# One block and one list of steps for the linear layer, the routing and the keys and values of a four-stage transformer kernel

## What is computed

```python
x = x + linear(layernorm(x), mask, weight, bias)      # weight (512 x 512) in 32x32 blocks; a block counts if its mask has a one
x = x + routed(layernorm(x), router, router_bias, expert_bias)
x = x + attention(layernorm(x), Wq, Wk_down, Wv_down, Wk_up, Wv_up, Wo)   # 32 query heads, 8 key heads, causal
x = x + feed_forward(layernorm(x), gate, up, down)

def routed(h):                                        # 64 experts, the 8 best are kept
    scores = softmax(h @ router.T + router_bias)
    w, idx = top_k(scores, 8)
    w_dense = zeros(T, 64).at[idx].add(w)
    return h * w.sum() + w_dense @ expert_bias
```

## Time and profile before

| | before |
|---|---|
| median of 3 runs | 1710.38 us |
| the profiled execution's own time | 1713.57 us |
| its span | 1711.8 us |
| PE busy | 1649.8 us (96%) |
| DVE / ACT / POOL busy | 1177.9 / 928.2 / 817.9 us |
| DMA | 114.99 MB, mean 67 GB/s |
| first linear matmul / last one over | 20.61 us / about 73.5 us |
| first routing transposes on PE | 79.39 us |
| first Z task on PE | 138.23 us |
| first matmul of the attention | 296.23 us |

### The profile page before, as it was taken

One profiled execution on the slowest core, in us unless ns is written; L12 is line 12 of the kernel. 1 busy time (PEld: TensorE's weight loads), 2 busy tenths in 40 slices (PEclk: granted clock), 3 DMA queues, 4 the chain that ended last, 5 costly groups with the idle time before them and its releaser, 6 DMA issues. The chain is left out here.

```text
span 1711.8 us, 26527 instructions
## 1 busy us (share of the span) xinstructions
PE 1649.8 (96%) x8298; PEld 1377.9 (80%) x8298; DVE 1177.9 (69%) x3102; ACT 928.2 (54%) x2456; POOL 817.9 (48%) x1203
## 2 busy tenths in 40 slices
PE   5878999999999999999999999999999899999999
PEld 4667897788888888888888888888888788877887
DVE  6775324767767767767767767776777677877776
ACT  3464435566556657647556656656656453424432
POOL 4633002445346346346346346445446198718752
PEclk9889999999999999999999999999999999999999
DMA  5200555211111111124111111111111022003111
GB/s 158 78 1 1 197 192 205 71 38 50 62 38 50 62 38 50 62 87 173 62 38 43 62 44 38 51 56 44 50 40 48 32 72 64 32 25 123 50 50 50
DMA packets 61338, 114.99 MB, mean 67 GB/s; under 512 B 5456, under 2 KB 23888, under 8 KB 57104
## 3 DMA queue, kind: packets, MB, share of 16 engines
q1 hardware_dynamic: 60304, 112.74, 19.9%
q10 hardware_dynamic: 896, 0.56, 0.2%
HBM read 84.97 MB, written 28.31 MB: 66 GB/s over the span
## 5 line engine op out<-in xcount | busy, mean ns | idle before, releaser
L1769 PE MATMUL ps_q<-kv_w_hi,o_hi 128*128 128x512 f32 x512 | 205.6, 402 | 3.0 <-DVE o_lo L131 3.0
L1769 PE MATMUL ps_q<-kv_w_lo,o_hi 128*128 128x512 f32 x512 | 201.3, 393 | 0.0
L1769 PE MATMUL ps_q<-kv_w_hi,o_lo 128*128 128x512 f32 x512 | 201.1, 393 | 0.0
L131 POOL TENSOR_TENSOR kv_w_lo<-w_raw,kv_w_hi 128x512 fp32r<-128x512 f32 x128 | 163.1, 1291 | 58.0 <-ACT kv_w_hi L126 58.0
L1711 PE MATMUL ps_q<-h_hi,kv_w_hi 128*128 128x512 f32 x448 | 182.3, 407 | 3.3 <-PEq L1056 1.4
L1711 PE MATMUL ps_q<-h_hi,kv_w_lo 128*128 128x512 f32 x448 | 175.3, 391 | 0.0
L1711 PE MATMUL ps_q<-h_lo,kv_w_hi 128*128 128x512 f32 x448 | 175.2, 391 | 0.0
L126 ACT ACTIVATE kv_w_hi<-w_raw 128x512 fp32r<-128x512 f32 (+1 forms) x240 | 126.6, 566 | 64.3 <-POOL w_raw L472 62.1
L126 ACT ACTIVATE o_hi<-ps_o 128x512 fp32r<-128x512 f32 x128 | 76.2, 595 | 130.0 <-PE ps_o L1751 129.9
L1354 ACT ACTIVATE prob<-prob,neg_max 128x128 f32<-128x128 f32 x256 | 100.3, 392 | 84.8 <-DVE neg_max L1511 84.7
L1298 POOL TENSOR_SCALAR prob<-prob,inv_sum 128x128 f32<-128x128 f32 x256 | 95.2, 372 | 106.0 <-DVE inv_sum L1516 105.8
(11 more groups left out here) (240 smaller groups left out, 4886.0 us busy)
## 6 DMA issues: line engine op xcount, KB each, us to landing
w_raw<-in_wq_g SPq DMA_DIRECT2D x16, 1024.0 KB, 4.8
w_raw<-in_wo_g SPq DMA_DIRECT2D x16, 1024.0 KB, 4.8
k_scratch<-kv_stage SPq DMA_DIRECT2D x32, 256.0 KB, 2.4
v_scratch<-kv_stage SPq DMA_DIRECT2D x32, 256.0 KB, 2.1
k_raw<-k_scratch SPq DMA_DIRECT2D x32, 256.0 KB, 3.4
v_raw<-v_scratch SPq DMA_DIRECT2D x32, 256.0 KB, 3.8
f_gate_raw<-in_gate_c SPq DMA_DIRECT2D x10, 512.0 KB, 4.8
f_up_raw<-in_up_c SPq DMA_DIRECT2D x10, 512.0 KB, 3.7
```

Of the source, the lines that this page charges most:

```text
L131: return dve.tensor_tensor(parts[LO], src, parts[HI].bitcast(F32), ALU.subtract)
L1769: done = pe.matmul(ps_q[:, half, :], o[b][i][:, half, h, :], wo[j][:, h, :], start=(h == 0 and m == 0), stop=(h == GROUP - 1 and m == 2))
```

## The change

- The linear layer becomes a class (`SparseLinear`), and linear layer, routing, keys and values are issued in one block (`first_stages`) from one list of steps, `head_steps`. Step s holds linear step s, routing step i = s - 6 (`FIRST_ROUTED`), piece p = s - 7 of the key and value weights, and some kv tasks. `ROUTED_GAP` is 0, so the routing's tiles follow each other without a pause. There are 31 steps.
- Within a step each engine does its linear part first, then the routing's, then the piece, then the tasks.
- The first tasks come at routing step 17 instead of 16, in groups of 2, 2, 3, 2, 2, 2, 3, 2: 18 tasks stand beside the routing instead of 9. They use banks 0 to 3, which the linear layer had.
- The start is written out by hand for tiles 0 and 1 (`pe_start`, `act_start`, `dve_start`, `pool_start`): tiles 0 and 1 are normalized and transposed among the steps that prepare the weight. The loads are issued in another order, all on SP: x tile 0, four mask chunks, x 1, four weight chunks, x 2, bias, x 3, the router's three, the other x tiles, then the pieces.
- The transposed linear tokens are kept in the room of `h3` instead of two buffers of their own.
- The pieces are 24 of 256 columns instead of 16 of 384, and POOL makes their low parts instead of DVE. DVE makes no `neg_mean` any more; the shift is one POOL instruction with the mean and the factor -1. The variance for the second norm moves from DVE to POOL, which had that for the third norm already.
- `weight_sum` and `combined` (two DVE instructions) become two POOL instructions.
- The operand sums of the attention's query product start at task V 0 of the first half instead of K 4, and steps 4 to 7 stand at the Z tasks of the second half. Stores of operand steps 3, 4 and 5 move behind those of `store_blocks`. The 32 K and V results of the first half are staged in `query.raw`, which is also the room of z, so ACT's first copy of the second half waits until all have been stored.

```diff
+FIRST_ROUTED = 6
+ROUTED_GAP = 0
+FIRST_PIECE = 7
...
+def head_steps():
+    ready = TILES // 2 + RoutedBias.DEPTH
+    group = (2, 2, 3, 2, 2, 2, 3) + (2,) * (RoutedBias.STEPS - ready - 7)
+    steps, n = [], 0
+    for s in range(FIRST_ROUTED + RoutedBias.STEPS):
+        i = s - FIRST_ROUTED
+        count = group[i - ready] if i >= ready else 0
+        steps.append((s, i, s - FIRST_PIECE, range(n, n + count)))
+        n += count
+    return steps, n
...
+                linear.pool_start(pool)
+                for s, i, p, _ in steps:
+                    if s >= 2:
+                        linear.pool_body(pool, s)
+                    if i == 0:
+                        routed.set_constants(pool, linear)
+                    routed.pool_body(pool, i)
+                    if 0 <= p < KV_PIECES:
+                        piece_lo_part(pool, p)
...
+    def pool_body(self, pool, i):
+        if 0 <= i - 2 < TILES:
+            t = i - 2
+            pool.wait_ge(self.h_done, t + 1)
+            pool.tensor_tensor(tile_of(self.x, t), tile_of(self.x, t), self.bias[:, :], ALU.add).then_inc(self.xb_done, 1)
+        if 0 <= i - 5 < TILES:
+            self.ln_next.variance(pool, i - 5)
+            self.ln_next.power(pool, i - 5)
+        if 2 <= i < TILES:
+            self.ln.power(pool, i)
...
     def power(self, pool, t):
         pool.wait_ge(self.ve_done, t + 1)
-        pool.tensor_tensor(self.factor(t, 0), self.ve[:, bass.ds(t, 1)], self.half, ALU.pow).then_inc(self.rstd_done, 1)
+        pool.tensor_tensor(self.factor(t, 0), self.ve[:, t:t + 1], self.half, ALU.pow).then_inc(self.rstd_done, 1)
         pool.wait_ge(self.rstd_done, t + 1)
-        pool.tensor_tensor(self.factor(t, 1), self.neg_mean[:, bass.ds(t, 1)], self.factor(t, 0), ALU.mult).then_inc(self.shift_done, 1)
+        pool.tensor_scalar(self.factor(t, 1), self.mv[:, t, 0:1], self.factor(t, 0), -1.0, ALU.mult, ALU.mult).then_inc(self.shift_done, 1)
...
-            dve.tensor_tensor(self.weight_sum[:, odd:odd + 1], self.top_sum[:, odd:odd + 1], self.inv_total[:, bass.ds(t3, 1)], ALU.mult).then_inc(self.sum_done, 1)
...
-            dve.scalar_tensor_tensor(self.combined[:, odd, :], self.ln.factors[:, bass.ds(t3, 1), :].rearrange("p t n -> p (t n)"),
-                                     self.weight_sum[:, odd:odd + 1], self.one_zero[:, :], ALU.mult, ALU.add).then_inc(self.combined_done, 1)
...
+            pool.tensor_scalar(self.combined[:, t % 2, :], self.ln.factors[:, t, :], self.top_sum[:, t % 2:t % 2 + 1],
+                               self.inv_total[:, t:t + 1], ALU.mult, ALU.mult).then_inc(self.scaled_factors, 1)
+            pool.wait_ge(self.scaled_factors, t + 1)
+            pool.tensor_scalar(self.combined[:, t % 2, 0:1], self.combined[:, t % 2, 0:1], 1.0, None, ALU.add).then_inc(self.combined_done, 1)
...
+                        if (quad, a) == (1, 0):
+                            for done in stored:
+                                act.wait_ge(done, 16 * (STAGED // STAGES))
```

More of the change, by code:

```diff
@@ L1064, in _ @@
             def _(sp):
+                linear.load(sp, lambda eng: weights.load(eng, *router_sources))
+                sp.wait_ge(linear.w_lo_done, KC)
+                for p in range(KV_PIECES):
+                    load_piece(sp, p)
                 for k, n in enumerate(stage_order):
@@ L1119, in task @@
                         operands.step_hi(act, step_at[n])
[L1121 removed]
+                linear.act_start(act)
+                for s, i, p, now in steps:
+                    if s >= 3:
+                        linear.act_body(act, s)
+                    if i == 0:
+                        act.wait_ge(linear.w_lo_done, KC)
+                    routed.act_body(act, i)
+                    if 0 <= p < KV_PIECES:
+                        piece_hi_part(act, p)
+                    for n in now:
+                        task(n)
+                for n in range(paired, len(tasks)):
+                    task(n)
             @block.vector
             def _(dve):
[L1125 removed]
                 def task(n):
@@ L1138, in task @@
                             dve.wait_ge(routed.lo_done, TILES)
+                            dve.wait_ge(piece_lo, KV_PIECES)
                         operands.step_sum(dve, step_at[n])
-                interleaved(dve, routed.dve_body, task)
+                linear.dve_start(dve)
+                for s, i, _, now in steps:
+                    if s >= 2:
+                        linear.dve_body(dve, s)
+                    if i == 0:
+                        routed.await_constants(dve)
+                    routed.dve_body(dve, i)
+                    for n in now:
+                        task(n)
+                for n in range(paired, len(tasks)):
+                    task(n)
             @block.tensor
             def _(pe):
-                routed.await_constants(pe)
+                awaited = set()
                 def task(n):
                     kind, quad, a, b = tasks[n]
+                    if kind in pieces_of and kind not in awaited:
+                        awaited.add(kind)
+                        pe.wait_ge(piece_lo, pieces_of[kind])
                     freed(pe, n)
@@ L1177, in task @@
                     last.then_inc(task_done, 1)
-                interleaved(pe, routed.pe_body, task)
+                linear.pe_start(pe)
+                for s, i, _, now in steps:
+                    if s >= 3:
+                        linear.pe_body(pe, s)
+                    if i == 0:
+                        routed.await_constants(pe)
+                        pe.wait_ge(linear.on_done, 1)
+                    routed.pe_body(pe, i)
+                    for n in now:
+                        task(n)
+                for n in range(paired, len(tasks)):
+                    task(n)
     return [(stored[k], 16 * (len(stage_order) // STAGES)) for k in range(STAGES)]
```

772 lines of the change are left out of this document (392 added, 380 removed).

## The result

| | before | after |
|---|---|---|
| median | 1710.26 us (4 runs, 1709.73 to 1714.35) | 1680.23 us (4 runs, 1679.63 to 1682.08) |
| ratio, 95% interval | | 0.9821 [0.9804, 0.9837] |
| span of the profiled execution | 1711.8 us | 1678.0 us |
| PE busy | 1649.8 us | 1631.0 us |
| first Z task on PE | 138.23 us | 121.53 us |

Runs of the kernel before fall near 1710 or near 1714.5 us; one of them that took 9347 us and one of e13 that took 3311 us are left out of all medians here.

A forecast was written before the change was run, and what follows sets the result against it. PE, busy 96% of the span, bounds the kernel, so the head pays only where PE idles or runs slowly. Step 22 ends 18.4 us earlier, step 23 loses 1.3, net 17: median 1710.38 to 1693.5, range 1685 to 1703.

The forecast's parts named there:

- So from 138.23 on the head is PE's own work, the same in both kernels: From the first Z task at 138.23 us on: PE's work unchanged, so only how early PE stands there counts.
- C and K tasks come two and three at a time ... which I cost at nothing: Behind step 23, tasks and routing sharing PE: grouped tasks on four banks change nothing, 1 us either way.
- Step 23, 1.3 us lost: Routing step without tasks ahead of the first Z: PE has 2.3 us of work, DVE 3.5, so 1.3 is lost.
- The common steps: Linear and routing work sharing steps: full steps 6.6 us each, 3 us added for waits, step 22 ending at 119.3.
- The start: Tiles 0 and 1: tile 1's linear matmuls end at 27.5 us, before 29.03, still at 0.43 apiece.
- POOL as the bound of the full steps: Steps 13 to 15: POOL becomes the slowest engine, 6.6 us a step, busy over 90%.
- A common step wins almost nothing; what is won is in the seams: Full common steps: 6.6 us, where linear layer and routing apart took 3.2 + 3.7 = 6.9.
- Hidden costs at 0: Second half's stores, ACT's wait at the first Z copy, and loads: cost 0; without cover 3 for operand stores, 2 for ACT.
- Rival C: Chance 0.09: slack is better, POOL's lines pack closer and the start is 3 us earlier; gain 25, 1685.
- D: Rival, chance 0.04: the kernel gets slower; its sign is a clock of 0.50 beyond 40 us.
- B: Rival, chance 0.14: in-order waiting adds 0.75 to each of steps 7 to 18; gain 8, 1702.
- E: Rival, chance 0.03: gain given back at the attention's start by operands or stores arriving last; 1710.

The follow-up runs named there:

- e13: Changed kernel with two more small DVE instructions in each routing step, results unused; 1679.4 us, 0.9803 of the kernel before.
- e4: Changed kernel with both address edits undone (small attention tiles first, HEAD_FILL = 40), leaving the schedule alone; 1687.7 us, 0.9858 of the kernel before.
- e7: Changed kernel with one key-and-value task behind each of routing steps 17 to 24 instead of 2 or 3; 1681.0 us, 0.9810 of the kernel before.
- e5: Changed kernel with POOL's two memsets of the routing's constants in step 3 instead of step 6; 1678.0 us, 0.9795 of the kernel before.
- e9: e5 with the 24 weight pieces moved to steps where POOL has time, none in 13 to 15 and 19 to 22; 1674.8 us, 0.9771 of before.
- e6: Changed kernel with FIRST_ROUTED = 21 instead of 6, so routing starts after the linear layer's last tile; 1703.2 us, 0.9941 of the kernel before.
- e3: Changed kernel with HEAD_FILL = 40 instead of 32, first-stage tiles behind it 32 bytes higher; 1683.8 us, 0.9838 of the kernel before.
- e12: Kernel before, own schedule, with attention's small tiles last and 224 bytes of filling aligning first-stage tiles to 512 bytes; 1701.4 us, 0.9934 of before.
- e10: Changed kernel with 64 bytes of filling ahead of prob_t and 64 more ahead of o; 1689.9 us (one run).
- e2: Changed kernel with the attention edit undone, three small tiles ahead of prob_t again; 1685.3 us, 0.9848 of the kernel before.
- e11: Changed kernel with 256 bytes of filling ahead of prob_t and 32 more ahead of o; 1686.1 us (one run).

## Why the prediction was wrong, step by step

- **"So from 138.23 on the head is PE's own work, the same in both kernels"** is the step that failed, and with it the unspoken term of nothing for the attention behind the head. The same instructions are not the same work: their operands' addresses moved. It cost the forecast 7.5 us (e4; 6 to 11 by the other ways of taking it), 2.4 in K and V and 5 in the attention. The edits of `HEAD_FILL` and in `attention` were there to be read, and neither was looked at.
- **"C and K tasks come two and three at a time ... which I cost at nothing"**: the 3.7 us of idle time of before, all waits for h_lo, went. e7 gives 2.2 of them to the groups; the other 1.5 have no experiment.
- **Step 23, 1.3 us lost**: 0.8, a wait for h1t.
- **The common steps**: right within 1 us in the sum (118.3 against 119.3), by luck: the errors cancel, and the first Z alone varies by 3 us with the clock. The start was over at 25.7 instead of 27.5 (24.2 where the granted clock of tile 1 was 1.00). Its terms for PE are those of the earlier trace rows: 29.03 - 25.83 = 3.2 us for a linear tile, 5.9 with a routing step's 2.7, and 0.43 us from matmul to matmul in tile 0, where the profile of before has a granted clock of 1.00 (20.60 to 25.80), so that no run shows why they are not 0.23 apart. In the changed kernel tile 1's matmuls are 0.43 apart from 22.19 to 23.47 and 0.23 from 24.30 on. The wait for the constants, which the diff shows on POOL in step 6, was overlooked and costs 2.3 us (e5). Steps 13 to 18 took 36.0 us instead of 37.3, since POOL's lead carried PE through the first two. Steps 19 to 22 took 18.1 instead of 15.9.
- **POOL as the bound of the full steps**: right (e9), 6.87 against 6.6.
- **"A common step wins almost nothing; what is won is in the seams"**: half right. By the estimate under e6, some 12 of 21 us go to the hole and the half clock, and 9 to the common steps: PE's steps 13 to 18 took 6.0 us each, where linear layer and routing apart took 6.9.
- **Hidden costs at 0**: right; no wait for a store or a load appears on PE behind the first Z.
- Rival C gave the nearest time, 1685. Half of its reason did come: the start was 1.8 us earlier than forecast, 3.3 where the granted clock was 1.00. The other half did not, since POOL's lines packed no closer, and the rest of its gain came from the addresses. D stood at 0.04; its sign, a clock of 0.50 for more than 40 us, did not come. For some us the clock did fall: from 33 to 40 us the granted clock is 0.76, behind the 2.25 us wait, and from 106 to 110 us 0.57. B and E did not appear.

The terms add up: 17 + 1.0 + 4.2 = 22.2 against 22.5 measured for the schedule (e4), and 7.5 for the addresses. With the schedule alone the time is 1687.7, inside the range; the addresses took it out. Without the idle time that went, they would not have done so: 1693.5 - 7.5 = 1686.

## What to carry to other kernels

A change that adds, drops or reorders allocations moves every tile behind them: compare the start addresses of TensorE's operands before calling a stage unchanged, and keep them on multiples of 512 bytes, which were fast in K, V and the attention's products (227 to 228 ns from matmul to matmul, against 230 to 233.3) and made no gain in the linear layer of the old schedule (256 was tried once, 228.6 ns). Overlap two stages whose bounds lie on different engines, then count the engine that collects the small work, step by step, and put what can wait (here the pieces) in the steps in which that engine is ahead. A one-time job in a list of steps, such as setting constants, belongs where its engine is idle, not at the step that first needs it.

## What the runs showed of the hardware

- In K, V, the product with prob_t and the output product, all back-to-back matmuls of 128x512 in fp32r, one follows the last after 227 to 228 ns when both operands begin on a multiple of 512 bytes (228.6 in the one case of 256), and after 230 to 233.3 ns when one of them, moving or stationary, begins 32, 64, 128 or 192 bytes behind a multiple of 256: 1.1 to 2.8%. Why is open. The linear layer's matmuls follow it in the changed kernel (229.2 ns, and 233.0 in e3 with the weight alone 32 bytes off), but not in the schedule before (229.8 with both operands off, 230.9 with both on in e12). Z's matmuls, whose tokens lie eight apart, take 245 ns in both kernels, with both operands on multiples of 1024.
- The granted clock of PE fell to 0.50 behind an idle time of 2.25 us in some executions and not in others. In the changed kernel's trace it is 0.50 from 35.80 to 37.93 and matmuls are 0.43 us apart there, then 0.23 again; in e3, e4, e7 and e10 it fell at the same place too, behind 2.21 to 2.24 us (0.76 from 33 to 40 us in each), and in e2 and e11 it stayed at 1.00 behind the same wait. In e5, where that wait is gone, the transposes at 30.68 and 33.89 take 0.60 us, as elsewhere at a granted clock of 1.00, where the changed kernel's at 34.46 take 1.11.
- The product of the chosen experts with their bias, the one of 128x512 in plain fp32 (L941 of before, reported as two matmuls), takes 0.86 us from its start at 120.48 to the next line's at 121.34; three fp32r passes of that size take 0.69 (0.23 apiece in the linear layer).
